# Attention with heads in pairs: two maxima and two exponentials in a row, ahead of the odd head's copy

## What is computed

```python
def _L0_xattn_ref(q, k, v, Wc, bc):          # k = v = ctx_512
    ...
    scale = 1.0 / math.sqrt(HEAD_DIM)
    scores = jnp.einsum('bghsd,bgtd->bghst', qh, kh) * scale
    probs = jax.nn.softmax(scores, axis=-1)
    out = jnp.einsum('bghst,bgtd->bghsd', probs, vh)
    out = out.transpose(0, 3, 1, 2, 4).reshape(b, s, D_MODEL)
    return out @ Wc.T + bc
...
x = x + _L0_xattn_ref(_layernorm(x, axis=-1), ctx_512, ctx_512, L0_xattn_Wc, L0_xattn_bc)
x = x + _L0_ffn_ref(_layernorm(x, axis=-1), L0_ffn_gate_kernel, L0_ffn_gate_proj, L0_ffn_up_proj, L0_ffn_down_proj)
```

## Time and profile before

| | |
|---|---|
| median of 3 runs | 9766.48 us (9765.42 to 9777.83) |
| the profiled execution | 9771.55 us, of which the span of the core is 9769.4 us |
| attention stage | about 60 to 3,060 us of the span |
| PE busy, share of the span | 94% |
| DVE, ACT, POOL busy | 66%, 43%, 54% |

### The profile page before, as it was taken

How to read it: one execution, slowest core, us unless ns; L and a number is a source line. 1 busy time by engine, 2 the same in 40 slices (tenths; PEclk the granted TensorE clock), 3 DMA queues, 4 the chain that set the end, 5 groups by cost and what they waited for, 6 DMA issues and landing times.

```text
span 9769.4 us, 175724 instructions
## 1 busy us (share of the span) xinstructions
PE 9218.2 (94%) x47664; PEld 7383.6 (76%) x47665; DVE 6401.2 (66%) x9152; ACT 4185.8 (43%) x6947; POOL 5238.8 (54%) x4825
## 2 busy tenths in 40 slices
PE   7888888888886899999999999999999999999999
PEld 4555555555554788888888888888888888888888
DVE  4555555555554676777766676767777666767676
ACT  5555555555553333333333333333333333333333
POOL 2333333333333665666655665656666565655564
PEclk9999999999998999999999999999999999999999
DMA  2111111111111455555544554545555445545554
GB/s 90 51 54 50 49 49 54 50 53 50 55 50 47 114 116 109 114 131 123 116 106 106 117 128 108 116 104 134 120 114 115 105 111 111 137 108 113 116 119 81
DMA packets 787086, 926.19 MB, mean 95 GB/s; under 512 B 403473, under 2 KB 600081, under 8 KB 786578
## 3 DMA queue, kind: packets, MB, share of 16 engines
q0 software_dynamic: 209920, 604.72, 28.9%
q1 hardware_dynamic: 430866, 165.82, 6.9%
q10 hardware_dynamic: 145920, 151.01, 4.8%
HBM read 1076.32 MB, written 376.45 MB: 149 GB/s over the span
## 4 chain that ended last, share of the span: by engine, by line
PE 63%; DVE 1%; issue 1%; ACTq 1%; ACT 0%; POOL 0%; DMA 0%; DVEq 0%; SPq 0%; POOLq 0%
PE bank L1590 42%; PE bank L1613 21%; DVE xT_lo L1498 0%; ACTq L1392 0%; ACTq L1384 0%; ACT xT_hi L1405 0%; POOL xg L1338 0%; DVE rows_out L1528 0%; DVE gu_lo L1504 0%; ACTq L1382 0%; DVE xT L1493 0%; DVE h L1516 0%; DVE h_lo L1521 0%; DVE h_hi L1519 0%; DMA entry_in<-slot_table 0%
## 5 line engine op out<-in xcount | busy, mean ns | idle before, releaser
L1338 POOL DMA_INDIRECT xg<-xn_rows,gather_row x2304 | 2953.2, 1282 | 1832.1 <-PE bank L1590 1346.8
L1590 PE MATMUL bank<-xT_hi,gu_hi 128*128 128x512 f32 (+2 forms) x6912 | 2559.9, 370 | 117.2 <-DVE xT_lo L1498 111.7
L1590 PE MATMUL bank<-xT_lo,gu_hi 128*128 128x512 f32 (+2 forms) x6912 | 2546.5, 368 | 0.0
L1590 PE MATMUL bank<-xT_hi,gu_lo 128*128 128x512 f32 (+2 forms) x6912 | 2546.2, 368 | 0.0
L1423 ACT ACTIVATE gated<-bank 128x512 f32<-128x512 f32 x432 | 258.7, 599 | 3027.3 <-PE bank L1590 3009.4
L1590 PEld LDWEIGHTS bank<-xT_hi,gu_hi 128*128 128x128 f32 x6912 | 1301.2, 188 | 303.0 <-issue 87.1
L1350 POOL DMA_INDIRECT out_rows<-rows_out,entry_now x576 | 1112.5, 1932 | 702.3 <-DVE rows_out L1528 410.6
L1590 PEld LDWEIGHTS bank<-xT_lo,gu_hi 128*128 128x128 f32 x6912 | 1301.8, 188 | 157.8
L1590 PEld LDWEIGHTS bank<-xT_hi,gu_lo 128*128 128x128 f32 x6912 | 1301.0, 188 | 158.4
L585 DVE TENSOR_REDUCE neg_max<-bank 128x1 f32<-128x512 f32 x1024 | 699.0, 683 | 961.6 <-PE bank L791 905.2
L1493 DVE STREAM_TRANSPOSE xT<-xg 128x512 f32<-128x512 f32 x1152 | 1284.1, 1155 | 9.0 <-DMA xg<-xn_rows,gather_row 8.4
(11 more groups left out here) (158 smaller groups left out, 12431.7 us busy)
## 6 DMA issues: line engine op xcount, KB each, us to landing
d_raw<-in_L_ffn_down_proj ACTq DMA_DIRECT2D x144, 1536.0 KB
gu_raw<-in_L_ffn_gate_proj ACTq DMA_DIRECT2D x145, 1024.0 KB
gu_raw<-in_L_ffn_up_proj ACTq DMA_DIRECT2D x145, 1024.0 KB
gu_raw<-in_L_ffn_gate_proj ACTq DMA_DIRECT2D x145, 512.0 KB
gu_raw<-in_L_ffn_up_proj ACTq DMA_DIRECT2D x145, 512.0 KB
xg<-xn_rows,gather_row POOLq DMA_INDIRECT x2304
x_t<-in_x SPq DMA_DIRECT2D x64, 512.0 KB, 4.7
inv_wide<-inverse_sums SPq DMA_DIRECT2D x512, 64.0 KB
```

The source lines that it names most:

```text
L1338: pool.indirect_dma_start(out=xg[:, m, :], out_offset=None, in_=quarter_rows, in_offset=bass.IndirectOffsetOnAxis(ap=gather_row[:, m:m + 1 ...
L1590: last = nc.tensor.matmul(bank[:, 0:cols], w[:, c, n, j * P:(j + 1) * P], v[:, c, 0:cols], start=(c == 0 and w is gu_hi and v is xT_hi), s ...
```

## The change

On ACT the exponentials of heads h+3 and h+4 are both written at odd h, ahead of `copy_probs(h)`; before, one stood at each step, behind the copy. On DVE the two maxima stand likewise together at the start of an odd step. PE's order is the same. Four further pieces move with them: `split_out_hi` from the steps 1, 5, 9, 13 to 0, 4, 8, 12, right behind those steps' copies; `normalise2` from step 3 to 2; `queries_hi` and `queries_lo` from step 7 to 8; and `keys_lo` one step later than `keys_hi`. `normalise_out` stands first in its step.

```diff
-            NEXT_STATS, NEXT_FACTORS, NEXT_NORM, NEXT_SPLIT, NEXT_QUERIES, NEXT_BIAS = (1, 2), 2, 6, 7, (10, 11, 12, 13), 8
+            NEXT_STATS, NEXT_FACTORS, NEXT_NORM, NEXT_SPLIT, NEXT_QUERIES, NEXT_BIAS = (1, 2), 2, 6, 8, (10, 11, 12, 13), 8
...
-            FACTORS2, NORM2, TRANSPOSE2, ROUTER, CHOOSE, MARK, TOP_EXP = 0, 3, (4, 5), 6, 7, (11, 13), 8
+            FACTORS2, NORM2, TRANSPOSE2, ROUTER, CHOOSE, MARK, TOP_EXP = 0, 2, (4, 5), 6, 7, (11, 13), 8
...
                     for h in range(H):
+                        if h % 2:
+                            for ahead in (h + AHEAD, h + AHEAD + 1):
+                                if ahead < H:
+                                    exponent(i, ahead)
+                                elif t.next:
+                                    exponent(i + 1, ahead - H)
                         if h % GROUP_HEADS != DVE_HEAD:
                             copy_probs(i, h)
-                        if h + AHEAD < H:
-                            exponent(i, h + AHEAD)
-                        elif t.next:
-                            exponent(i + 1, h + AHEAD - H)
-                        if h in OUT_SPLIT and (t.back1 or not OUT_SPLIT[h][0]):
-                            split_out_hi(i - OUT_SPLIT[h][0], OUT_SPLIT[h][1])
+                        if h in OUT_NORM and (t.back1 or not OUT_NORM[h][0]):
+                            split_out_hi(i - OUT_NORM[h][0], OUT_NORM[h][1])
...
-                        if h + AHEAD < H:
-                            maximum(i, h + AHEAD)
-                        elif t.next:
-                            maximum(i + 1, h + AHEAD - H)
+                        if h % 2:
+                            for ahead in (h + AHEAD, h + AHEAD + 1):
+                                if ahead < H:
+                                    maximum(i, ahead)
+                                elif t.next:
+                                    maximum(i + 1, ahead - H)
+                        if h in OUT_NORM and (t.back1 or not OUT_NORM[h][0]):
+                            normalise_out(i - OUT_NORM[h][0], OUT_NORM[h][1])
...
-                        if h in OUT_SPLIT and (t.back1 or not OUT_SPLIT[h][0]):
-                            split_out_lo(i - OUT_SPLIT[h][0], OUT_SPLIT[h][1])
-                        for b, g in groups_at(t, h, KEYS):
+                        if h - 1 in OUT_NORM and (t.back1 or not OUT_NORM[h - 1][0]):
+                            split_out_lo(i - OUT_NORM[h - 1][0], OUT_NORM[h - 1][1])
+                        for b, g in groups_at(t, h - 1, KEYS):
                             keys_lo(b, g)
```

More of the change, by code:

```diff
@@ L216, in moe_block @@
             OUT_NORM = {0: (1, 2), 4: (1, 3), 8: (0, 0), 12: (0, 1)}
-            OUT_SPLIT = {h + 1: back_group for h, back_group in OUT_NORM.items()}
             DVE_HEAD = 1
@@ L548, in _ @@
                     copy_queries(0, 0, n)
-                for h in range(AHEAD):
+                for h in range(AHEAD + 1):
                     exponent(0, h)
@@ L703, in tile @@
                             copy_probs(i, h)
-                        if h in OUT_NORM and (t.back1 or not OUT_NORM[h][0]):
-                            normalise_out(i - OUT_NORM[h][0], OUT_NORM[h][1])
-                        if h in OUT_SPLIT and (t.back1 or not OUT_SPLIT[h][0]):
-                            split_out_lo(i - OUT_SPLIT[h][0], OUT_SPLIT[h][1])
-                        for b, g in groups_at(t, h, KEYS):
+                        if h - 1 in OUT_NORM and (t.back1 or not OUT_NORM[h - 1][0]):
+                            split_out_lo(i - OUT_NORM[h - 1][0], OUT_NORM[h - 1][1])
+                        for b, g in groups_at(t, h - 1, KEYS):
                             keys_lo(b, g)
```

## The result

The changed kernel takes 9378.94 us (median of 4 runs, 9373.67 to 9384.30); the kernel before, beside it, 9766.96 us. The ratio is 0.960, with a 95% interval of 0.9584 to 0.9617: 388 us less. The forecast was 9,366 us.

What follows compares the result with a forecast made beforehand. PE was taken to bound the attention stage, with gaps. Savings of 248 - 7 + 70 + 65 + 24 = 400 us from 9771.55 gave 9,371, less 5 for the median: 9,366 us; range 9,340 to 9,495.

Steps and rivals of the forecast that it cites:

- The bound: Attention stage: PE bounds it, with gaps, busy 884 of 1,000 us; its three kinds of waits make 341 us.
- The scores' chain: Each pair in attention: scores, maxima, exponentials, next scores; 1.25 us to spare, so 248 us of waits fall to 7.
- `normalise2`: PE's wait for the second norm in attention: moved from step 3 to 2, all 70 us go.
- The clock and the drain: Attention stage: low clock behind long waits gone, 65 us; PE draining at 296 waits, 0.08 each, gone, 24 us.
- The loop's turn: PE's waits before a transpose at the turn of attention's loop: 22 us stay.
- the sum of 400: Total us expected to go from the attention stage: 248 - 7 + 70 + 65 + 24.
- Rival 1: Low part of the output on DVE waits through both POOL operations: up to 48 us lost, 9,414 us; chance 0.15.
- Rival 2: New chain at step 8, output's high part, queries, POOL, PE, makes PE wait: 9,493 us; chance 0.12.
- Rival 3: PE's waits in attention only change their name: a third of the gain lost, 9,499 us; chance 0.13.
- Rival 4: Odd head's copy behind both exponentials delays transposes if the second starts after 4.1: slower, 9,827 us; chance 0.03.

Runs made afterwards that it cites:

- pair_only: The changed kernel with pairs of maxima and exponentials kept but the four other moves undone: 9689.77 us, ratio 0.9866 to the kernel before.
- pair_norm2: The changed kernel with the moves of queries, output's high part and keys_lo undone, normalise2 kept at step 2: 9414.79 us, ratio 0.9642 to the kernel before.
- exp_only: The changed kernel with each maximum back at its old step, ACT's order as changed: 9854.90 us, ratio 1.0037 to the kernel before.
- bias_late: The kernel before with POOL's add_bias at step 11 instead of 8, nothing else: 9635.95 us, ratio 0.9874 to the kernel before.

## Why the prediction was right, point by point

- **The bound.** PE's waits in the attention stage were the thing to remove. Measured: PE busy from 884 to 980 of 1,000 us; a tile takes 40.4 us (the router's rank matmuls of two tiles, L882, start at 1420.91 and 1461.27), forecast 41.
- **The scores' chain** (exponentials at 1.72 and 2.42, 1.25 us to spare). Measured 1.72 and 2.39 in the rows above. The waits left are 5.1 us; 7 were forecast, as 0.4 us in each of 16 pairs, but they are four waits, three of them (4.9 us) in the program's first pairs, so that this number is near by luck.
- **`normalise2`.** 70 us forecast, 69.4 measured (70.3 to 0.9). I had it as one term among four; pair_only against pair_norm2 shows that without that move it is not 70 us but some 221 us of the stage that are missing. The prediction priced the step's own wait of before, not what it would have become behind the pair.
- **The clock and the drain**, 65 and 24 us. The waits of PE of the attention stage add up to 357.9 us before (with 11.5 for the router, 3.5 and 2.3 for the queries) and to some 59 us now, 299 us less. The stage is 390 us shorter, so 91 us are clock and drain; 89 were forecast. The granted clock parts them: its lower level holds for 130 us less (143.5 to 13.5), which at half speed is worth up to 65 us and leaves 26 or more for the drain. The 65 and 24 of the sum fit, as an estimate.
- **The loop's turn.** 22 us were to stay. It is 16.7 us under another name (a head's transposes wait for ACT's copy), but there is a new wait of 10.0 us for the product of group 2, whose engine DVE comes back late from the turn, as in this one (DVE, then PE):

```profile
382.68 0.42 DVE L610 TENSOR_TENSOR o_norm<-bank,inv_wide 128x256 f32<-128x256 f32 x1 [6.02 <-issue]
```
```profile
383.25 0.63 PE L778 MATMUL bank<-ident,ctx_sb 128*128 128x128 f32 x4 [2.03 <-DVE o_norm L610]
```

With 4.8 us more for the router's input and 5.6 less at the turn, this is 9 of the 13 us by which the sum of 400 was too high. The step that was missing is that DVE and ACT pass the turn too, with their own delay.
- **Rival 1**, the low part behind both POOL operations: no. It takes 1.52 us and is let in between the two (a middle value of 1.53 in the 63 tiles where they meet). The prediction took 0 "since between two POOL operations in a row there is a gap of issue"; the rows show no gap (the first ends at 1443.61, the second starts at 1443.58), so that reason did not hold. That DVE's request is the older one fits, but no run tests it. The rule of the Trainium skill, "SBUF - State Buffer", section "SBUF: two separate sides", of a lock held for a whole instruction agrees with both the 2.39 us of before and the 1.52 us of now, and bias_late gives the price of the clash: 125 us in the kernel before.
- **Rival 2**, the chain at step 8: on the first chip no wait (queries for POOL: 5.1 us in two places, of which the longest, 3.5, was there before). The lengths came out as worked out: high part at 0.10, POOL from 1.65 to 4.03.
- **Rival 3**, waits that change their name: true of pair_only and exp_only, not of the whole change.
- **Rival 4**, slower by a late second exponential: not here. exp_only shows it, but by another way than I wrote: not the transposes two steps on, but the router's input, queued on ACT behind the waiting exponential. The point from which that decides is earlier than the 4.1 us I gave. PE was ready at 1509.42 (1511.38 less its wait of 1.96); the copy needs 0.64 from its start to the matmuls, the exponential ahead of it 0.68, and the scores started at 1505.83, so by these rows it is about 2.3. The exponential came at 4.2.

## What to carry to other kernels

When a consumer frees a pair of buffers, look at when the second of its two readers gets its turn, and on which engine something else stands in front of it; here moving one maximum forward on DVE was worth 217 us alone. A reordering that puts a waiting instruction ahead of a ready one needs what it waits for moved forward as well: here the half on DVE alone gained, and the half on ACT alone was slower than nothing. And before the sum is trusted, list the second-tightest chains too: extra work of 0.6 us that the main chain had room for cost 80 us by way of the others.

## What the runs showed of the hardware

- The same program gained 388 us on one chip and 314 us on another, where the kernel before was only 52 us slower. The 62 us between the last exponentials are about what PE's waits have more, 43.4 us without a named cause and 19.5 us for the exponentials, in tiles in which DVE started up to 3 us and ACT 1 us after their data were there. Moving the queries' split (one operation on ACT, one on POOL) a step forward took DVE's waits of this kind from 233.6 to 9.3 us. The cause is open.
- DVE's two maxima back to back take 1.29 us, not twice 0.69: in these rows an instruction overlaps the end of the one ahead by 0.09.
- POOL's second wide operation grew from 2.41 to 2.56 us where DVE was let in between, and DVE's operation took 1.52 us instead of the 2.39 of before.
- In exp_only PE was at the lower clock right behind a wait of 1.96 us (16 matmuls in 3.62 instead of 1.97 us). Waits of about this length stood there in nearly every tile, but in 27 of 64 the 16 matmuls took 1.97 us all the same. The mean clock of the second thousand us was 0.94, the lowest of all kernels in which nothing was added.
